# Second FFN of a macaron block: rows gathered per tile by GpSimd, against rows scattered to slots in DRAM and loaded by SyncE

## Chip, core and metric

One core of one Trainium2 chip. The metric is the device time of one execution in microseconds (us), the median of 3 runs. Five engines have programs of their own: TensorE (PE in the trace, its weight loads PEld), VectorE (DVE), ScalarE (ACT), GpSimd (POOL) and SyncE (SP, here only an issuer of DMAs).

## What is computed

The input x is 2 x 2048 tokens of 256 features in fp32, 4096 tokens in all. Three steps follow each other:

```python
x = x + 0.5 * ffn(layernorm(x))
x = x + attention(layernorm(x))
x = x + 0.5 * ffn(layernorm(x))

def ffn(xf):                      # xf: (4096, 256)
    scores = softmax(xf @ gate_w.T)            # 16 experts in 4 groups
    # two groups by the sum of their two best of (scores + gate_b), in them the two best experts
    weights, idx = the two chosen of scores
    h = silu(einsum('td,edi->tei', xf, We1) + be1) * (einsum('td,edi->tei', xf, We3) + be3)
    y = sum over the two experts of weight * (h @ We2 + be2)        # i = 128
    z = silu(xf @ ws1 + bs1) * (xf @ ws3 + bs3) @ ws2 + bs2          # shared, 256 wide
    return y + z
```

The attention is causal with 16 heads; a head's scores are products of six-element vectors (exterior products of two projections of four), and its values are 16 wide.

## The kernel before

Every token's residual row stays in SBUF (`x_res`, 32 tiles of 128 tokens; in blocks of `BT` = 4 tiles, so 8 blocks). The kernel is one program per engine, written out by hand; semaphores alone order the engines, and each engine and each DMA queue works its instructions in the order in which they stand.

**Attention** (`attend`) runs in 8 groups of 48 strips. For each strip TensorE makes scores (L1877), ScalarE their exponentials (L2017), GpSimd masks the strips on the diagonal (L2027), and TensorE multiplies with the values (L1903). Query chunks `qc` of 512 tokens end at fixed strips. Steps of other work are put between strips by tables of (group, strip) numbers: `turn_at`, `logits_at`, `count_at` (the second FFN's routing), `late_at` (turns of the last block of the lines, from the stage ahead of attention), `PROJECT_7` and `PROJECT_6_LATE` (the output projection L1917, whose product VectorE adds to `x_res` in L2097). `GATE` is 4, the first group in which the finished first half of the tokens may be normalized and routed. Normalized rows go to DRAM (`xn_rows`), a block of 4 tiles in a transfer (512 KB).

**The second FFN** (`ffn_by_halves`) works in two halves of 2048 tokens. Its slots: each (token, k) pair has a slot number, sorted by expert with every expert's share filled up to whole tiles of 128, which gives 47 tiles a half, 94 **turns**. `Routing.place` computes an offset per expert (`offset`) and the slot of each pair (`sum_slots`). A tile needs the tokens of its slots, so the map must be inverted: VectorE marks for each pair its row in the tile (`mark_rows`, L1152) and its tile (`mark_tiles`, L1158; `mark_of_pairs`, L1163; `scale_tiles`, L1167), TensorE multiplies the marks (`invert`, 32 small matmuls accumulated), and VectorE turns the product into token numbers (`name_tokens`). For half 0 the marks are made in the last attention group (`add_among_marks`), for half 1 inside turns 4 to 23, with the inversion at turn 26.

The loop over turns, as each engine sees it: GpSimd gathers the 128 rows of a turn from `xn_rows` with an indirect DMA (`bring`, L2499) into a ring of 16 tiles and, from turn 40, 8 more lent from `f_region`, the buffer of the marks. TensorE turns the rows (L2379), multiplies them with the expert's two up weights (L2391, 8 matmuls a turn) and the product down (L2403). ScalarE and VectorE copy, add biases and apply the gate between them; VectorE also copies each tile's expert weights by a register index (`take_weights`). SyncE stores each result tile to DRAM (`y_half`, L2292) from a ring of `ROUND` = 4. Once half 0 is stored, GpSimd gathers its results back for each token (`bring_back`, L2507), two gathers a tile of tokens, 32 for half 0 among the gathers of turns from turn 77 on (`BACK_TURN`), and VectorE adds them (`combine`, at the turns in `COMBINE_AT`). Half 1's results are gathered after the last turn, in the tail, together with the shared part (`shared_up`, L2560); `out` is stored by SyncE (L2296).

## Time and profile before

| what | value |
|---|---|
| median of 3 runs (lowest, highest) | 1233.25 us (1230.09, 1234.88) |
| the profiled execution's own time | 1235.22 us |
| its span in the trace | 1233.5 us |
| TensorE busy | 1046.1 us, 85% |
| VectorE busy | 772.3 us, 63% |
| ScalarE busy | 873.3 us, 71% |
| GpSimd busy | 457.8 us, 37% |

"Busy" counts the time of instructions that compute, for GpSimd also the time in which it writes the descriptors of an indirect DMA. It is an average over stages; which engine bounds a stage is read from that stage's window.

How the rows further down are read. A row of windows has, in this order: from and to (us from the start of the span), their length, then the busy us of PE, PEld, DVE, ACT and POOL with the number of records in brackets, the granted TensorE clock as a share of full speed, the mean busy share of the 16 DMA engines, and the GB/s that they moved. With a line chosen, only PE and PEld remain, which are the engines that run it. A row of the timeline has its start, its busy us, the engine, the line, output<-input with shapes, and in square brackets how long the engine was idle before it and what released it; "remote" is a release by something the trace doesn't name, "issue" is no wait that it shows. A row of groups has count, busy us, mean ns, and after the second bar the group's idle time with its releasers. A row of DMA queues has packets, MB and the share of 16 engines' span; a row of DMA issues ends with the size and the median us from issue to landing.

### The profile page before, as it was taken

The numbers are of one execution on the slowest core, as the hardware profiler recorded it, in microseconds if no ns is written. First come the engines' busy times: TensorE is split into PE (matmuls) and PEld (weight loads), VectorE is DVE, ScalarE is ACT, GpSimd is POOL, SyncE is SP. The second block draws the span as 40 slices with busy tenths as digits, with TensorE's granted clock in tenths as the row PEclk, the third lists the DMA queues.
The fourth block names the chain that finished last, engine by engine and source line by source line (L and its number), as shares of the span: only waits on it lengthen the run. The fifth ranks groups of instructions, "written<-read, shape, count | busy, mean of one in ns | idle before, by whom it ended". The sixth has DMA issues, their size and how long they took to land.

```text
span 1233.5 us, 23530 instructions
## 1 busy us (share of the span) xinstructions
PE 1046.1 (85%) x7487; PEld 570.4 (46%) x7487; DVE 772.3 (63%) x1565; ACT 873.3 (71%) x1250; POOL 457.8 (37%) x675
## 2 busy tenths in 40 slices
PE   3998999877887688988898989897999886967894
PEld 3457888744555212222222222221245685957752
DVE  6897777665997423444355565675786873645845
ACT  4246776624878999999999999999972463745610
POOL 1004555375630324331313234313133446564363
PEclk8999999998989799999999999999999997998997
DMA  8902544443756211010101130201009443443453
GB/s 294 279 4 78 161 152 156 130 127 108 219 176 213 88 31 52 18 52 18 52 18 53 35 104 19 74 15 52 2 31 318 127 137 124 155 137 114 131 167 120
DMA packets 125717, 133.79 MB, mean 108 GB/s; under 512 B 13224, under 2 KB 111888, under 8 KB 125616
## 3 DMA queue, kind: packets, MB, share of 16 engines
q1 hardware_dynamic: 109056, 90.95, 23.2%
q0 software_dynamic: 14448, 39.47, 11.1%
q10 hardware_dynamic: 2112, 2.10, 0.5%
q8 instruction: 55, 0.90, 0.3%
q14 instruction: 46, 0.38, 0.1%
HBM read 80.43 MB, written 52.04 MB: 107 GB/s over the span
## 4 chain that ended last, share of the span: by engine, by line
PE 30%; ACT 23%; issue 14%; DVE 7%; another core or an unknown queue 4%; DVEq 1%; ACTq 0%
ACT wide L2017 19%; PE banks L1903 6%; PE banks L2391 5%; PE banks L2316 3%; PE banks L2403 2%; PE banks L1877 2%; PE banks L2325 2%; PE banks L1433 2%; PE banks L1436 1%; PE banks L2379 1%; PE banks L1362 1%; DVEq L2599 1%; PE banks L1420 1%; PE banks L1917 1%
## 5 line engine op out<-in xcount | busy, mean ns | idle before, releaser
L2017 ACT ACTIVATE wide<-banks 128x1536 f32<-128x1536 f32 (+1 forms) x384 | 492.6, 1475 | 9.9 <-PE banks L1877 8.5
L1903 PE MATMUL banks<-wide,attn_attend_v_now 128*32 128x512 f32 (+3 forms) x2560 | 290.9, 546 | 1.9 <-ACT wide L2017 1.0
L2027 POOL TENSOR_SCALAR_AFFINE_SELECT wide<-wide 128x256 f32<-128x256 f32 (+1 forms) x320 | 115.3, 389 | 398.9 <-ACT wide L2017 396.4
L1877 PE MATMUL banks<-attn_attend_q_now,attn_attend_k_now 32*128 32x512 f16 (+3 forms) x1280 | 151.6, 357 | 55.6 <-ACT wide L2017 52.6
L1877 PEld LDWEIGHTS banks<-attn_attend_q_now,attn_attend_k_now 32*128 32x128 f16 x1280 | 38.8, 91 | 292.7 <-ACT wide L2017 243.2
L2391 PE MATMUL banks<-f_xnt 128*128 128x128 f32 x752 | 108.3, 290 | 39.0 <-ACT f_xnt L2476 19.2
L651 POOL DMA_INDIRECT f_region<-xn_rows,f_token_of x79 | 77.3, 978 | 137.1 <-DVE f_token_of L882 84.8
L2391 PEld LDWEIGHTS banks<-f_xnt 128*128 128x128 f32 x752 | 97.3, 202 | 46.5 <-ACT f_xnt L2469 25.3
L2072 DVE COPY sums<-banks 128x512 f32<-128x512 f32 x32 | 22.1, 692 | 141.9 <-PE banks L1903 141.6
L2077 DVE RECIPROCAL below<-below 128x512 f32<-128x512 f32 x32 | 107.3, 3353 | 1.1
L2499 POOL DMA_INDIRECT last_rows_in<-xn_rows,f_spare x72 | 69.6, 967 | 78.1 <-DVE f_stage L2560 24.5
L520 PE MATMUL banks<-f_region,wide 128*128 128x128 f32 x632 | 86.5, 280 | 6.4 <-issue 3.4
L1903 PEld LDWEIGHTS banks<-wide,attn_attend_v_now 128*32 128x32 f32 x2560 | 57.0, 109 | 75.1 <-issue 72.7
L520 PEld LDWEIGHTS banks<-f_region,wide 128*128 128x128 f32 x632 | 78.0, 194 | 10.1 <-issue 6.7
L2469 ACT ACTIVATE f_xnt<-last_w_all 128x514 f32 x94 | 59.4, 632 | 30.2 <-issue 23.7
L2483 ACT ACTIVATE f_xnt<-banks,f_xnt 128x128 f32<-128x128 f32 x94 | 34.3, 364 | 55.4 <-PE banks L2391 37.6
L1341 POOL DMA_INDIRECT f_region<-y_slots,attn_lines_rows_of x64 | 64.0, 1000 | 23.6 <-issue 17.1
L2610 DVE TENSOR_TENSOR f_xnt<-banks,last_w_down 128x256 f32<-128x256 f32 x94 | 39.4, 419 | 47.7 <-PE banks L2403 27.9
L619 ACT ACTIVATE wide<-f_w_all 128x514 f32 x79 | 49.9, 632 | 26.7 <-issue 23.6
L2403 PE MATMUL banks<-last_w_down,f_more 128*128 128x256 f32 x188 | 59.1, 397 | 1.0 <-DVE f_more L2617 1.0
L2097 DVE TENSOR_TENSOR x_res<-banks,x_res 128x512 f32<-128x512 f32 x30 | 20.7, 690 | 61.9 <-PE banks L1917 61.8
L2602 DVE COPY last_w_down<-last_w_all 128x512 f32 x94 | 41.5, 441 | 27.3 <-issue 23.8
(365 smaller groups left out, 1799.6 us busy)
## 6 DMA issues: line engine op xcount, KB each, us to landing
y_half<-f_xnt SPq DMA_DIRECT2D x94, 128.0 KB
y_slots<-wide SPq DMA_DIRECT2D x79, 128.0 KB
attn_v<-f_more SPq DMA_DIRECT2D x32, 256.0 KB
attn_attend_v_now<-attn_v SPq DMA_DIRECT2D x32, 256.0 KB, 3.3
x_res<-L_attn_x SPq DMA_DIRECT2D x8, 512.0 KB, 7.6
xn_rows<-f_w_all SPq DMA_DIRECT2D x8, 512.0 KB, 4.5
attn_q<-attn_lines_q_out SPq DMA_DIRECT2D x8, 512.0 KB
attn_k<-attn_lines_k_out SPq DMA_DIRECT2D x8, 512.0 KB
```

The source lines that it names most:

```text
L520: last = pe.matmul(bank[2 + m][:, f * P:(f + 1) * P], w_up[:, at, col_at:col_at + INTER], rows_t[:, m, c * P:(c + 1) * P], start=(c == 0), ...
L651: pool.indirect_dma_start(out=rows_in[:, n % ROUND, :], out_offset=None, in_=xn_rows, in_offset=bass.IndirectOffsetOnAxis(ap=token_of[:, n ...
L1341: pool.indirect_dma_start(out=back[:, q, j, k, :], out_offset=None, in_=y_slots, in_offset=bass.IndirectOffsetOnAxis(ap=rows_of[:, q, j, k ...
L1877: last = pe.matmul(score[i % SLOTS][:, j, column:column + columns(u)], k_now[rows, kt * P:(kt + 1) * P], q_now[rows, qc * QW + c0:(qc + 1) ...
L1903: last = pe.matmul(out_bank[qc][rows, c0:QW], v_now[:, kt, rows], probs[:, place, column:column + columns(u)], start=(kt == 0), stop=(u == ...
L2017: act.activation(probs_flat[:, at:at + width_of[i]], score_flat[i % SLOTS][:, 0:width_of[i]], ACT.Exp, scale=SCALE).then_inc(sem.exp_done, 1)
L2027: pool.affine_select(out=part, in_=part, compare_op=ALU.is_ge, fill=0.0, base=0, pattern=[[0, part.shape[1]], [1, P]], channel_multiplier= ...
L2077: dve.reciprocal(below[:], below[:]).then_inc(sem.chain_step, 1)
L2391: last = pe.matmul(bank[2 + m][:, f * P:(f + 1) * P], w_up[:, at, col_at:col_at + INTER], rows_t[:, m, c * P:(c + 1) * P], start=(c == 0), ...
L2403: pe.matmul(bank[4 + m][:, 0:D], prod_t[:, at, :], w_down[:, at, 0:D], start=True, stop=True).then_inc(sem.y_done, 1)
L2469: act.activation(w_up[:, n % ROUND, :], w_all[:, bass.ds(expert, 1), 0:UP].rearrange("p o f -> p (o f)"), ACT.Copy).then_inc(sem.up_kept, 1)
L2499: pool.indirect_dma_start(out=rows_in(n), out_offset=None, in_=xn_rows, in_offset=bass.IndirectOffsetOnAxis(ap=s.token_of[:, place_of_turn ...
```

## The change

The inversion goes. In its place the rows themselves are scattered: GpSimd writes the 128 rows of a tile of tokens to their slots in DRAM (`x_slots0`, `x_slots1`, 47 x 128 rows of 1 KB each), one indirect DMA for each of the 32 (tile, k) pairs of a half (`send`), and SyncE loads each turn's 128 rows from there with one plain transfer (`load_rows`), into a ring of 8 tiles, the next one behind each store of a result. The slots that no pair fills must hold something finite: SyncE clears both tensors with two transfers of zeros ahead of the loads of attention group 2 (`clear`). The normalized rows are loaded back from `xn_rows` into `f_region` ahead of the scatters (`fetch_rows`: four transfers of 512 KB a half, for half 1 at turn 4). Half 0 is sent in bursts of 7, 14, 4, 4 and 3 (`SENT`), the first two in the last attention group, the others ahead of the loop; half 1 follows at once in one burst of 32. The gathers of half 0's results then stand alone in the loop (turn 57 on for `combine`, one every other turn). The addition of the shared bias to half 1 moves from behind the loop, as 4 instructions, into turns 7 to 21, as 8. In attention, slots of half 0 are computed a group earlier, and turns, projections and copies move to other strips.

```diff
-    def place_pairs(self, dve, half):
-        for k in range(TOPK):
-            self.sum_slots(dve, k)
-        self.split_slots(dve)
...
-    def mark_rows(self, dve, first, pairs):
-        s = self.s
-        some = slice(first, first + pairs)
-        row_id = self.core.row_id[:].rearrange("p (o m) -> p o m", o=1).to_broadcast([P, pairs, P])
-        row_of = s.row_of[:, some].rearrange("p (q o) -> p q o", o=1).to_broadcast([P, pairs, P])
-        dve.tensor_tensor(s.row_hot[:, some, :], row_id, row_of, ALU.is_equal)
...
-    def name_tokens(self, dve, half, bank):
...
+    def clear(self, sp, x_slots):
+        sp.wait_ge(self.s.sem.zeros_made, 1)
+        for slots in x_slots:
+            sp.dma_start(dma_rows(slots), self.s.zeros.rearrange("p (o d) -> p o d", o=1).to_broadcast([P, HALF_TURNS, D])
+                         ).then_inc(self.s.sem.cleared, 16)
+
+    def fetch_rows(self, sp, half, xn_rows):
+
         s = self.s
-        dve.wait_ge(s.sem.inverted, half + 1)
-        dve.tensor_scalar(s.token_f, bank[:, HS:2 * HS], float(P), float(half * HT * P - 1), ALU.mult, ALU.add)
-        self.step(dve, dve.scalar_tensor_tensor(s.empty_f, bank[:, 0:HS], 0.0, self.core.part_one[:].to_broadcast([P, HS]), ALU.is_equal, ALU.mult))
-        self.step(dve, dve.tensor_tensor(s.token_f, s.token_f, bank[:, 0:HS], ALU.add))
-        dve.tensor_tensor(s.token_of[:, half * HS:(half + 1) * HS], s.token_f, s.empty_f, ALU.add).then_inc(s.sem.tokens_ready, 1)
+        sp.wait_ge(s.sem.slots_ready, half + 1)
+        if half == 0:
+            for q in range(2):
+                sp.wait_ge(s.stored[q], 16 * HB // 2)
+        else:
+            for q in range(2):
+                sp.wait_ge(s.stored[q], 16 * (BLOCKS - 2) // 2)
+            sp.wait_ge(s.stored[2], 16 * 2)
+            sp.wait_ge(s.sem.sent, 16 * HP)
+        for b in range(HB):
+            first = half * HT + b * BT
+            sp.dma_start(s.rows_out[:, b * BT:(b + 1) * BT, :], dma_rows(xn_rows)[:, first:first + BT, :]).then_inc(s.fetched[b], 16)
+
+    def send(self, pool, half, first, end, x_slots):
+
+        s = self.s
+        if half == 0 and first == 0:
+            pool.wait_ge(s.sem.cleared, 16 * 2)
+        for pair in range(first, end):
+            t, k = pair // TOPK, pair % TOPK
+            if pair == first or pair % (BT * TOPK) == 0:
+                pool.wait_ge(s.fetched[t // BT], 16 * (half + 1))
+            at = half * HT + t
+            pool.indirect_dma_start(out=x_slots[half], out_offset=bass.IndirectOffsetOnAxis(ap=self.core.slots[:, at, k:k + 1], axis=0),
+                                    in_=s.rows_out[:, t, :], in_offset=None).then_inc(s.sem.sent, 16)
...
-    def invert(self, pe, half, bank):
-        s = self.s
-        pe.wait_ge(s.sem.hot_ready, half + 1)
-        for q in range(HP):
-            last = pe.matmul(bank[:, 0:2 * HS], s.row_hot[:, q, :], s.tile_hot[:, q, :, :].rearrange("p a s -> p (a s)"),
-                             start=(q == 0), stop=(q == HP - 1))
-        last.then_inc(s.sem.inverted, 1)
...
-PROJECT_7, PROJECT_6, PROJECT_6_LATE = (22, 25), (34, 38, 42, 45), (39, 41, 43, 45)
+PROJECT_7, PROJECT_6, PROJECT_LATE = (22, 25), (34, 38, 42, 45), (25, 28, 38, 41, 43, 45)
...
-               (GATE + 1, 10): (2, 0), (GATE + 1, 13): (2, 1), (GATE + 1, 18): (3, 0), (GATE + 1, 20): (3, 1)}
-    weights_at, logits_at, logits_turn_at, count_at, exp_at = (GATE, 34), (GATE + 1, 34), (GATE + 1, 38), (GATE + 2, 45), (GATE + 2, 4)
...
+               (GATE + 1, 10): (2, 0), (GATE + 1, 13): (2, 1), (GATE + 1, 21): (3, 0), (GATE + 1, 23): (3, 1)}
+    weights_at, logits_at, logits_turn_at, count_at, exp_at = (GATE, 34), (GATE + 1, 34), (GATE + 1, 36), (GATE + 2, 42), (GATE + 2, 4)
...
-    late_at = {(0, 3): 0, (0, 5): 1, (0, 9): 2, (0, 11): 3}
...
+    late_at = {(0, 18): 0, (0, 20): 1, (0, 22): 2, (0, 25): 3}
+    late_bank = banks[:, 7, :]
+    copied_at = (0, 4)
...
+            if g == 2:
+                routing.clear(sp, x_slots)
...
+        routing.fetch_rows(sp, 0, xn_rows)
...
+                if u == last_of[0] and g == 1:
+                    pool.memset(second.zeros, 0.0).then_inc(second.sem.zeros_made, 1)
+                if u == last_of[1] and g == GATE + 3:
+                    routing.send(pool, 0, 0, SENT[0], x_slots)
...
                 if u == last_of[2] and g == GATE + 3:
                     routing.take_root(pool, HB, BT)
+                    routing.send(pool, 0, SENT[0], SENT[1], x_slots)
...
                 routing.weigh(dve, 0)
                 routing.keep_counts(dve, 0, rest_bank(count_at[1]))
                 dve.sem_inc(sem.rest_kept, 1)
-            elif g == GATE + 3 and qc == 0:
                 routing.place(dve, 0)
-            elif g == GATE + 3 and qc == 1:
                 routing.name_experts(dve, 0)
...
-        def add_among_marks(two):
+        def add_last_chunks(two):
 
             routing.normalize(dve, HB)
             add_half(two, 1, 0)
-            routing.mark_rows(dve, 0, HP)
-            routing.mark_tiles(dve)
             add_half(two, 1, 1)
             sum_block(two, 1)
-            routing.mark_tokens(dve)
             add_half(two, 2, 0)
...
-ROWS, LENT, LENT_FROM = 16, 8, 40
+SENT = (7, 21, 25, 29)
+ROWS = 8
...
+        def load_rows(n):
+            if n >= ROWS:
+                sp.wait_ge(sem.rows_turned, n - ROWS + 1)
+            half, at = n // HALF_TURNS, n % HALF_TURNS * P
+            sp.dma_start(rows_in[:, n % ROWS, :], x_slots[half][at:at + P, :]).then_inc(row_loaded[n % ROWS], 16)
+
+        sp.wait_ge(before.proj_added, ends.adds)
+        sp.wait_ge(first.sent, 16 * HP)
+        for n in range(ROWS):
+            load_rows(n)
         for n in range(TURNS):
+            if n == 4:
+                routing.fetch_rows(sp, 1, xn_rows)
+            if n + ROWS == HALF_TURNS:
+                sp.wait_ge(first.sent, 16 * 2 * HP)
             sp.wait_ge(sem.y_ready, n + 1)
             sp.dma_start(y_halves[n // HALF_TURNS][n % HALF_TURNS * P:(n % HALF_TURNS + 1) * P, :], y_rows[:, n % ROUND, :]).then_inc(row_stored[n % ROUND], 16)
+            if n + ROWS < TURNS:
+                load_rows(n + ROWS)
...
-            if n == INVERT_AT:
-                routing.invert(pe, 1, bank[6])
...
         routing.take_root(pool, HB + 1, BT)
+        routing.send(pool, 0, SENT[1], SENT[2], x_slots)
         routing.take_root(pool, HB + 2, BT)
-        pool.wait_ge(first.tokens_ready, 1)
-        pool.wait_ge(before.pv_done, ends.values)
-        for n in range(4):
...
-        for n in range(ROWS, TURNS):
-            if n == LENT_FROM:
-                pool.wait_ge(first.inverted, 2)
-            if n == HALF_TURNS:
-                pool.wait_ge(first.tokens_ready, 2)
-            bring(n)
...
-            pair = n - BACK_TURN
-            if pair == 0:
-                for q in range(ROUND):
-                    pool.wait_ge(row_stored[q], stored_by(q, HALF_TURNS))
-            if pair >= 0:
-                bring_back(pair // TOPK, pair % TOPK)
-        for pair in range(TURNS - BACK_TURN, HP):
-            bring_back(pair // TOPK, pair % TOPK)
+        pool.wait_ge(s.stored[0], 16 * (BLOCKS - 2) // 2)
+        pool.wait_ge(s.stored[1], 16 * (BLOCKS - 2) // 2)
+        for t in range(HT):
+            for k in range(TOPK):
+                bring_back(t, k)
...
+        dve.wait_ge(first.sent, 16 * HP)
...
+        def add_shared_bias(i):
+            pair = x[:, HT + 2 * i:HT + 2 * i + 2, :]
+            dve.tensor_tensor(pair, pair, s.bs2.rearrange("p (o d) -> p o d", o=1).to_broadcast([P, 2, D]), ALU.add).then_inc(first.bs2_added, 1)
...
-        SOME = HP // 8
-        rows_at = {n: SOME * i for i, n in enumerate((6, 7, 9, 10, 12, 13, 15, 16))}
+        bs2_at = {7 + 2 * i: i for i in range(HT // 2)}
         for n in range(TURNS + 3):
             if n in (2, 3):
                 routing.sum_slots(dve, n - 2)
             if n == 4:
-                routing.split_slots(dve)
-            if n == 5:
                 routing.name_experts(dve, 1)
-            if n in rows_at:
-                routing.mark_rows(dve, rows_at[n], SOME)
-            if n in (18, 19):
-                routing.mark_tiles(dve, (n - 18) * HP // 2, HP // 2)
-            if n in (20, 21):
-                routing.mark_of_pairs(dve, (n - 20) * HP // 2, HP // 2)
-            if n == 22:
-                routing.scale_tiles(dve, 0, HP // 2)
-            if n == 23:
-                routing.scale_tiles(dve, HP // 2, HP // 2).then_inc(first.hot_ready, 1)
-            if n == INVERT_AT + 3:
-                routing.name_tokens(dve, 1, bank[6])
+            if n in bs2_at:
+                add_shared_bias(bs2_at[n])
...
-        for b in range(HB, BLOCKS):
-            part = x[:, b * BT:(b + 1) * BT, :]
-            dve.tensor_tensor(part, part, s.bs2.rearrange("p (o d) -> p o d", o=1).to_broadcast([P, BT, D]), ALU.add).then_inc(first.bs2_added, 1)
-        dve.wait_ge(first.bs2_added, BLOCKS)
+        dve.wait_ge(first.bs2_added, HB + HT // 2)
...
-INVERT_AT, BACK_FIRST, BACK_RING = 26, 4, 2 * BT
+BACK_FIRST, BACK_RING = 4, 2 * BT
...
-BACK_TURN = HALF_TURNS + ROWS + LENT + 6
-COMBINE_AT = (61, 64, 67, 70, 73, 76, 79, 82, 84, 85, 87, 88, 90, 92, 93, 95)
+COMBINE_AT = range(HALF_TURNS + 10, HALF_TURNS + 10 + 2 * HT, 2)
```

Three places show how instructions move. GpSimd from the last masks of attention to the first results gathered back (`f_spare` is the root of the variance, `f_region` and `last_rows_in` the two parts of the ring), before:

```order
L2027 AFFINE_SELECT wide<-wide 128x128
L1021 TENSOR_TENSOR f_spare<-f_spare 128x4 x2
L2499 DMA last_rows_in<-xn_rows,f_spare 128x256 x4
L1021 TENSOR_TENSOR f_spare<-f_spare 128x4
L2499 DMA last_rows_in<-xn_rows,f_spare 128x256 x36
L2499 DMA f_region<-xn_rows,f_spare 128x256 x8
L2499 DMA last_rows_in<-xn_rows,f_spare 128x256 x16
L2499 DMA f_region<-xn_rows,f_spare 128x256 x8
L2499 DMA last_rows_in<-xn_rows,f_spare 128x256 x6
L2507 DMA f_stage<-y_half,slots 128x256
```

and after:

```order
L2011 AFFINE_SELECT wide<-wide 128x128
L1018 TENSOR_TENSOR f_spare<-f_spare 128x4
L1172 DMA x_slots<-f_region,slots 6016x256 x4
L1018 TENSOR_TENSOR f_spare<-f_spare 128x4
L1172 DMA x_slots<-f_region,slots 6016x256 x4
L1018 TENSOR_TENSOR f_spare<-f_spare 128x4
L1172 DMA x_slots<-f_region,slots 6016x256 x35
L2479 DMA f_stage<-y_half,slots 128x256 x32
L2479 DMA last_w_all<-y_half,slots 128x256 x32
```

The 94 gathers of rows are gone; the last 3 scatters of half 0 and the 32 of half 1 stand in one run, and the 64 result gathers follow with nothing between them.

VectorE in the last attention group, between the last chunk's normalization and the statistics of the added block, before:

```order
L1036 TENSOR_SCALAR f_stage<-x_res,f_spare 128x256 x4
L2097 TENSOR_TENSOR x_res<-banks,x_res 128x512
L1152 TENSOR_TENSOR f_region<-row_id,f_spare 128x4096
L1158 TENSOR_TENSOR f_region<-tile_id,f_spare 128x32x48
L2097 TENSOR_TENSOR x_res<-banks,x_res 128x512
L152 BN_STATS parts<-x_res 128x6 x4
```

and after:

```order
L1033 TENSOR_SCALAR f_stage<-x_res,f_spare 128x256 x4
L2086 TENSOR_TENSOR x_res<-banks,x_res 128x512 x2
L152 BN_STATS parts<-x_res 128x6 x4
L1002 TENSOR_TENSOR f_spare<-parts 128x4
L1003 TENSOR_TENSOR f_spare<-parts 128x4
```

The two marks between the two additions are gone, so the additions follow each other.

SyncE from the last expert weights (`last_w_all`) to the output, before:

```order
L2288 DMA last_w_all<-L_ffn_We 128x16x256
L2289 DMA last_w_all<-L_ffn_be 128x16x256
L2292 DMA y_half<-f_xnt 128x256 x94
L2296 DMA out<-x_res 128x4x256 x7
L2296 DMA out<-x_res 128x2x256
```

and after, up to the store of turn 4:

```order
L2253 DMA last_w_all<-L_ffn_We 128x16x256
L2254 DMA last_w_all<-L_ffn_be 128x16x256
L2260 DMA last_rows_in<-x_slots 128x256 x8
L2272 DMA y_half<-f_xnt 128x256
L2260 DMA last_rows_in<-x_slots 128x256
L2272 DMA y_half<-f_xnt 128x256
L2260 DMA last_rows_in<-x_slots 128x256
L2272 DMA y_half<-f_xnt 128x256
L2260 DMA last_rows_in<-x_slots 128x256
L2272 DMA y_half<-f_xnt 128x256
L2260 DMA last_rows_in<-x_slots 128x256
L1160 DMA f_region<-xn_rows 128x4x256 x4
```

Loads of rows now alternate with the stores of results in one queue, and the four reloads of half 1 stand ahead of the store of turn 4 and all behind it.

## Rows read from the trace of the kernel before

**Rows 1.** Windows by stage, columns as told in the section on the profile.
```profile
403.00:915.00 512.00, 450.70 (x4075) 124.40 (x4075) 271.33 (x381) 498.19 (x392) 149.69 (x337) 0.98 0.13 40
915.00:966.80 51.80, 50.43 (x194) 29.85 (x193) 39.56 (x91) 15.47 (x25) 16.67 (x17) 1.00 0.75 241
966.80:1015.00 48.20, 40.48 (x299) 35.88 (x297) 38.90 (x106) 31.02 (x76) 23.52 (x24) 1.00 0.41 127
1015.00:1050.00 35.00, 23.68 (x162) 20.99 (x161) 12.86 (x38) 14.08 (x34) 19.44 (x21) 0.80 0.37 117
1050.00:1080.00 30.00, 29.44 (x225) 27.03 (x225) 20.46 (x55) 21.24 (x54) 18.39 (x20) 1.00 0.52 164
1080.00:1140.00 60.00, 43.20 (x283) 38.44 (x282) 30.68 (x83) 29.52 (x71) 32.25 (x34) 0.91 0.42 126
1140.00:1172.40 32.40, 28.78 (x201) 24.65 (x200) 26.30 (x73) 19.63 (x49) 12.65 (x13) 1.00 0.43 129
1172.40:1233.50 61.10, 44.09 (x128) 24.78 (x126) 30.62 (x54) 5.39 (x8) 31.14 (x32) 0.86 0.46 143
```

**Rows 2.** The same windows of the loop for line 2391 alone (8 records a turn).
```profile
966.80:1015.00 48.20, 27.27 (x200) 24.25 (x200) 1.00 0.41 127
1015.00:1050.00 35.00, 14.51 (x86) 13.36 (x87) 0.80 0.37 117
1050.00:1080.00 30.00, 19.79 (x149) 17.95 (x149) 1.00 0.52 164
1080.00:1140.00 60.00, 28.73 (x190) 25.98 (x190) 0.91 0.42 126
1140.00:1172.40 32.40, 18.01 (x132) 15.79 (x130) 1.00 0.43 129
```

**Rows 3.** The chain that ended last, two turns: start, us, what.
```profile
1057.28 0.89 PE banks L2391 x8
...
1058.82 0.89 PE banks L2391 x8
```

**Rows 4.** GpSimd's groups in the loop: busy us, mean ns, idle before and its releasers.
```profile
L2499 POOL DMA_INDIRECT last_rows_in<-xn_rows,f_spare x56 | 54.2, 968 | 41.5 <-PE banks L2379 24.2 <-issue 10.8 <-DVE x_res L2552 3.4
```

**Rows 5.** Timeline of one stall: start, us, engine, line, [idle before <-releaser].
```profile
1036.48 0.95 POOL L2499 DMA_INDIRECT last_rows_in<-xn_rows,f_spare  x1 [0.30 <-issue]
...
1038.75 0.37 ACT L2483 ACTIVATE f_xnt<-banks,f_xnt 128x128 f32<-128x128 f32 x1 [4.20 <-remote]
1038.79 0.42 DVE L2610 TENSOR_TENSOR f_xnt<-banks,last_w_down 128x256 f32<-128x256 f32 x1 [3.62 <-remote]
```

**Rows 6.** Timeline of VectorE, a mark inside a turn.
```profile
999.80 0.95 DVE L1158 TENSOR_TENSOR f_region<-tile_id,f_spare 128x768 bf16<-128x768 bf16 x1
```

**Rows 7.** Timeline of the last attention group.
```profile
884.23 1.02 POOL L1021 TENSOR_TENSOR f_spare<-f_spare 128x4 f32<-128x4 f32 x1 [3.87 <-DVE f_spare L1011]
...
895.00 4.41 DVE L1152 TENSOR_TENSOR f_region<-row_id,f_spare 128x4096 bf16<-128x4096 bf16 x1
...
901.98 0.65 POOL L2027 TENSOR_SCALAR_AFFINE_SELECT wide<-wide 128x256 f32<-128x256 f32 x2 [16.73 <-ACT wide L2017]
...
907.69 1.10 PE L1917 MATMUL banks<-attend_w_o,heads 128*128 128x256 f32 x4 [1.86 <-DVE x_res L2097]
...
909.16 2.99 ACT L2017 ACTIVATE wide<-banks 128x1536 f32<-128x1536 f32 x2 [1.28 <-PE banks L1877]
```

**Rows 8.** DMA: the hardware queue, and a wide window under full load.
```profile
q1 hardware_dynamic: 109056, 90.95, 23.2%
...
925.00:962.00 37.00, 36.35 (x133) 19.94 (x132) 26.30 (x67) 8.57 (x14) 9.98 (x11) 1.00 0.94 303
...
xn_rows<-f_w_all SPq DMA_DIRECT2D x8, 512.0 KB, 4.5
```

**Rows 9.** SyncE's queue between attention groups 2 and 3.
```profile
539.73 29.92 SPq L1786 DMA_DIRECT2D attn_attend_q_now<-attn_q  x4
```

**Rows 10.** Timeline of VectorE's longest wait in the tail.
```profile
1205.87 0.75 DVE L2560 SCALAR_TENSOR_TENSOR f_stage<-banks,last_bs,f_more 128x512 f32<-128x512 f32 x1 [12.82 <-remote]
```

118 lines of the change are left out of this document (35 added, 83 removed).

## Prediction, written before the changed kernel was run

> **What bounds the kernel now.** I read the windows by stage first [rows 1]; one row is one stretch, and its first columns are the busy time of TensorE, its weight loads, VectorE, ScalarE and GpSimd. Attention (403 to 915) is ScalarE's: 498.19 busy of 512.00 us. From 915 to the start of the loop over turns TensorE is busy 50.43 of 51.80 us. The loop itself (five windows, 205.6 us) belongs to nobody: at best TensorE fills 29.44 of 30.00 us, at worst 23.68 of 35.00. The reader is to see that the loop has one good window and four bad ones with the same work per turn.
>
> How much is lost there comes from line 2391 alone, 8 records a turn [rows 2]: 200, 86, 149, 190 and 132 records are 25, 10.75, 18.6, 23.75 and 16.5 turns. Undisturbed, two turns stand 1058.82 - 1057.28 = 1.54 us apart in the chain of waits [rows 3]. At 1.545 us a turn the windows would take 38.6, 16.6, 28.8, 36.7 and 25.5 us; they take 9.6, 18.4, 1.2, 23.3 and 6.9 us more, **59.4 us lost in all**. (94 turns at 1.545 us are 145.2 us.)
>
> What goes with the losses is GpSimd. A gather occupies it 0.95 us and 0.30 us pass to the next [rows 5], so at most one goes out per 1.25 us. In the good window it issues 20 [rows 1] in 30 us, one a turn, each held back by the ring. In the window 1015 to 1050 it issues 21, all but a few of them back to back, and from 1080 to 1140 34, because gathers for the turns and gathers of finished results share it: 2 x 1.25 = 2.5 us a turn against 1.545. In such a burst ScalarE and VectorE then stand still together for 4.20 and 3.62 us on something the trace calls remote, although TensorE has nothing long to do [rows 5]; the granted clock of the stretch falls to 0.80 between the two levels of 1.2 and 2.4 GHz [rows 1], after TensorE had stood idle. That is a correlation and not yet a cause: bursts lose 18.4/21 = 0.88 us per indirect transfer in one window and 23.3/34 = 0.69 in the other, paced ones 1.2/20 = 0.06.
>
> The tail (61.1 us) has the same picture: a burst of gathers, and VectorE waits 12.82 us on remote [rows 10]. The change leaves that burst in place.
>
> **The change part by part.** *GpSimd in the loop.* Before, 78 of the 94 row gathers (56 of them into the own ring [rows 4], 22 into the lent one) and 32 result gathers fall into the loop, 110 x 1.25 = 138 us of issue. After, 32 scatters and 32 gathers, 64 x 1.25 = 80 us. No scatter is in the trace; the nearest row is the gather of the same 128 rows of 1 KB, 0.95 us [rows 5], and I take that for it (both ends: a descriptor list of 128 rows is built either way, and a scatter at twice the price, 64 + 80 = 144 us in all, would only restore the old load). Result gathers no longer alternate with row gathers: their pairs take 2.5 us per two turns (3.1 us). So the 23.3 and 6.9 us of the last two windows shrink. I leave 8 us for them: the first eight go as one burst (8 x 0.69 = 5.5), the 24 paced ones cost 24 x 0.06 = 1.4, and 1 for the two additions, about 1 us per two turns, that VectorE must place in slack.
>
> *The burst of 32 scatters* for the second half replaces the one at 1015 to 1050. Priced like a paced transfer it loses 32 x 0.06 = 2 us, like the gather burst 32 x 0.88 = 28 us. The 18.4 us it replaces include the inversion on TensorE, whose 32 small matmuls go. I take 16 us, 0.5 a scatter, in between: it is a burst like those, but no turn waits for a row that GpSimd has yet to fetch. SyncE also puts 2.1 MB of row reloads (4 x 512 KB) ahead of the stores of turn 4 and later. The queue moved 90.95 MB in 23.2% of 1233.5 us, 318 GB/s while busy [rows 8], so that is 6.6 us; the ring of four result rows covers 6.2 us less the landing, so 3 us.
>
> *VectorE in the loop* loses its marks: a mark of tiles takes 0.95 us in a turn [rows 6] and four such turns overrun; of the 9.6 us in the first window I leave 5 for the offset steps, which stay. Eight additions of the shared bias come in at turns 7 to 21, of 128x512 each, one per two turns; the nearest row is the mark's 0.95 us. The cover is what VectorE has free, 9.5 us in 18.6 turns of the good window [rows 1, 2], about 1 us in two turns; without it they cost 8 x 0.95 = 7.6 us. The third window keeps its 1.2, and 4 us stay for what I cannot name. Loop after: 5 + 16 + 3 + 1 + 8 + 4 = 37 us lost instead of 59, **-22 us**.
>
> *Last attention group.* The marks of half 0 stand on VectorE between additions: 4.41 us for the first alone; TensorE's projection then waits 1.86 us for an addition and ScalarE idles 1.28 us [rows 7]. Gone: **-1.3 us**. GpSimd gets 7 and 14 scatters here. The 14 follow the root that ends at 885.25 and take 17.5 us, to 902.75; the masks start at 901.98 after 16.73 us of idleness [rows 7]. They come 0.8 us late and are needed some strips later, so 0. The moved steps in attention (turns of the last line block, projections, logits, counts) keep their number: they take from the 512.00 - 498.19 = 13.8 us that ScalarE is not busy, **-1 us** (0 to -3).
>
> *Clearing.* SyncE writes 2 x 47 x 128 rows of 1 KB, 12.3 MB, after the last load for group 2, whose issue begins at 539.73 [rows 9]. At 318 GB/s this is 39 us; the window 925 to 962 shows 303 GB/s with TensorE busy 36.35 of 37.00 us under it [rows 8]. A group lasts 512/8 = 64 us, and group 2 has just begun, so group 3 starts at about 602 and the clear is hidden with some 20 us to spare: 0.
>
> *Before the loop and in the tail.* TensorE's matmuls between 915 and 967 stay; the inversion of half 0 goes, but beside it VectorE's last chunk runs anyway: 0. The loads of the first eight tiles queue behind the expert weights and wait for all 32 scatters of half 0: 0, at worst 3. In the tail four bias additions of 128x1024 leave VectorE while TensorE has the matmuls of two blocks ahead: 0. If that cover were gone they would give up to 4 x 2 x 0.95 = 7.6.
>
> Sum: 22 + 1.3 + 1 = 24 us off the span of 1233.5, so 1209.2; the profiled run took 1235.2, 2.0 above the median of 1233.25, so the same 24 us off the median give **1209 us**.
>
> **Two rules against the rows.** The good window has a DMA share of 0.52 and the burst window 0.37 [rows 1]: the engines are not full where the loop stands still. The Trainium skill, DMA: Bandwidth & Descriptors, section on queues, rings and completion order, says that each DMA engine takes turns between the queues that have work, packet by packet. By that rule a burst of GpSimd's would hardly hold up SyncE's stores, and the rows do not agree, unless the wait is for something else. The same page, section on issuing engines that are not separate DMA queues, says that starting transfers from another engine saves only the time to start them. The trace agrees that this time is what GpSimd spends; for the bytes it speaks against the change.
>
> **The rivals.** *A, bursts like the paced transfers.* The low DMA share in the burst window speaks for it, the 4.20 us waits against. The 16 and 3 us shrink to 2: 1192 us. (The page's taking of turns would have this outcome.)
>
> *B, the DMA engines become the bound of the loop.* Loop transfers of 128 KB: before 94 stores + 78 + 32 gathers = 204, after 94 stores + 94 loads + 32 scatters + 32 gathers + 16 of reload = 268, 35 MB, 110 us at 318 GB/s in a loop of 182. For: loads and stores share one queue and the rings hold eight rows instead of 16 to 24. Against: 110 is below 145. If each fetched row and store comes late for a third of the turns by half a microsecond, 15 us return: 1224 us. (The second rule of the page points here.)
>
> *C, scatters of half 0 hurt attention or the start.* 21 transfers at 0.5 us stalls of ScalarE's stream, partly hidden: +6, 1215 us. Against: ScalarE and TensorE wait for no DMA in the last group.
>
> *D, the clear is too slow, the other side.* Writes of 512 KB to DRAM land 4.5 us after issue [rows 8], 117 GB/s with the latency in it. At that rate the clear lasts 105 us and the loads of group 3 stand behind it: 105 + 540 = 645 against 602, 43 us of stall, 1252 us. It stalls from 12.3 MB / 62 us = 199 GB/s down; it turns the sign from 12.3 / (62 + 24) = 143 GB/s.
>
> **How the numbers follow.** Main case 0.48 (1199 to 1222), A 0.20, B 0.14, C 0.10, D 0.08. The range from 1186 to 1230 takes in the main case, A, B and C, whose bounds reach 2 and 28 us for the burst; D lies outside. Half a per cent (6 us, about what can be told from no change) ends at 1227: faster 0.48 + 0.20 + 0.10 and half of B, 0.85; within 0.5% the rest of B, 0.07; slower D, 0.08.
>
> **What would show it.** The loop from its first row transpose to its last product takes about 182 us instead of 205.6; GpSimd shows 32 transfers of 0.95 us in a row early in it, and stalls on remote lie inside that burst and not between turns 47 and 94. The third attention group keeps its length, DMA share near 1 for 39 us at 540. VectorE's first additions in group 7 have no gap over 2 us. The prediction is wrong if a scatter occupies GpSimd much longer than 0.95 us, if TensorE waits for a row that SyncE loaded, or if group 3 starts late.

## The result: 1246.3 us against 1232.2, slower by 1.0%

Four runs of the changed kernel take 1244.04 to 1248.74 us, median 1246.33; the kernel before, four runs now, has 1232.2. The ratio is 1.0099, 95% interval 1.0073 to 1.0125. The forecast was 1209. On other chips the sign is the other one (0.990, below); this section is about the first kind of chip, on whose trace the prediction was made.

The profiled execution took 1247.99 us, span 1246.3, 12.8 more than before. Four landmarks split these 12.8. Attention, from its first to its last exponential, took 506.9 us (403.8 to 910.7) and takes 516.6 (405.3 to 921.9): **+9.7**. From there to the first row transpose of the loop it was 56.2 and is 58.6: **+2.4**. The loop took 205.1 (966.9 to the last product at 1172.0) and takes 204.1 (980.5 to 1184.6): **-1.0**. The tail was 61.5 and is 61.7, and attention starts 1.5 later. The forecast was 37 us below this span: 12 of them are attention (-2.3 us was forecast), 21 the loop (-22).

Windows of the changed kernel, with the columns of [rows 1]: the last attention group, the stretch before the loop, six parts of the loop, the tail.

```profile
861.00:922.00 61.00, 48.49 (x374) 13.05 (x374) 23.83 (x50) 45.43 (x35) 31.54 (x47) 0.86 0.13 46
922.00:980.00 58.00, 54.48 (x214) 32.51 (x207) 40.46 (x95) 16.93 (x27) 11.76 (x12) 0.94 0.70 224
980.40:998.00 17.60, 14.64 (x109) 12.81 (x107) 14.10 (x41) 11.55 (x28) 0.00 (x0) 1.00 0.28 90
998.00:1045.00 47.00, 15.62 (x75) 13.22 (x73) 8.35 (x21) 7.03 (x17) 30.64 (x32) 0.66 0.47 163
1045.00:1104.00 59.00, 58.26 (x430) 54.21 (x431) 41.90 (x113) 43.20 (x111) 0.00 (x0) 0.95 0.54 162
1104.00:1120.00 16.00, 10.72 (x64) 9.61 (x63) 5.65 (x16) 6.66 (x17) 7.73 (x8) 0.79 0.55 163
1120.00:1163.00 43.00, 40.88 (x305) 36.60 (x305) 36.97 (x101) 30.40 (x76) 23.52 (x24) 1.00 0.76 216
1163.00:1185.00 22.00, 21.33 (x156) 18.90 (x155) 17.24 (x48) 14.67 (x37) 0.32 (x1) 1.00 0.50 151
1185.00:1246.30 61.30, 44.48 (x129) 24.80 (x127) 25.71 (x49) 5.39 (x8) 30.49 (x32) 0.88 0.46 143
```

The same six parts of the loop for the up product alone (L2371, 8 records a turn), as in [rows 2]:

```profile
980.40:998.00 17.60, 9.93 (x72) 8.72 (x72) 1.00 0.28 90
998.00:1045.00 47.00, 9.84 (x48) 9.08 (x48) 0.66 0.47 163
1045.00:1104.00 59.00, 39.96 (x288) 36.66 (x288) 0.95 0.54 162
1104.00:1120.00 16.00, 7.14 (x41) 6.67 (x42) 0.79 0.55 163
1120.00:1163.00 43.00, 27.32 (x204) 24.59 (x205) 1.00 0.76 216
1163.00:1185.00 22.00, 13.65 (x103) 12.13 (x101) 1.00 0.50 151
```

At 1.545 us a turn they lose 3.7, **37.7**, 3.4, 8.1, 3.6 and 2.1 us. The 47 us in which GpSimd issues the 32 scatters of half 1 hold 6 turns. GpSimd is at 30.64 us there, TensorE at 15.62 and VectorE and ScalarE under 9, the DMA engines at 0.47. In the 59 us behind it, with nothing on GpSimd, TensorE is busy 58.26.

What the engines wait for inside that run is in its timeline (start, us, engine, line, what, [idle before it and releaser]):

```profile
1008.59 1.72 PE L2371 MATMUL banks<-f_xnt 128*128 128x128 f32 x8
...
1010.14 0.60 PE L2383 MATMUL banks<-last_w_down,f_more 128*128 128x256 f32 x2
...
1010.58 0.38 PE L2359 MATMUL banks<-ident,last_rows_in 128*128 128x128 f32 x2
...
1013.17 0.38 ACT L2454 ACTIVATE f_xnt<-banks 128x256 f32<-128x256 f32 x1 [4.34 <-issue]
...
1015.50 1.06 PE L2383 MATMUL banks<-last_w_down,f_more 128*128 128x256 f32 x2
...
1016.35 0.61 PE L2359 MATMUL banks<-ident,last_rows_in 128*128 128x128 f32 x2
...
1025.84 0.37 ACT L2461 ACTIVATE f_xnt<-banks,f_xnt 128x128 f32<-128x128 f32 x1 [12.28 <-remote]
...
1031.43 0.42 DVE L2568 TENSOR_TENSOR f_xnt<-banks,last_w_down 128x256 f32<-128x256 f32 x1 [18.64 <-remote]
...
1031.88 0.32 SPq L2272 DMA_DIRECT2D y_half<-f_xnt  x1
...
1037.04 0.38 ACT L2454 ACTIVATE f_xnt<-banks 128x256 f32<-128x256 f32 x1 [9.60 <-remote]
1037.53 2.05 PE L2371 MATMUL banks<-f_xnt 128*128 128x128 f32 x8 [20.57 <-issue]
1038.08 0.96 POOL L1172 DMA_INDIRECT x_slots<-f_region,slots  x1 [0.30 <-issue]
```

Each of these lines has its 94 turns in the trace, so a product and its reader can be matched by counting. The up product of turn 12 was done at 1010.3, and ScalarE, which reads it, starts at 1025.84, 15.5 us later. The down product of turn 10 was done at 1010.7, and VectorE starts on it at 1031.43, 20.7 us later. The transpose of turn 14 was done at 1011.0, and ScalarE starts on it at 1037.04, 26.1 us later. (What TensorE did at 1015.50 and 1016.35 belongs to turns 11 and 15 and was read later still.) The releases come 5.6 us apart (1025.84, 1031.43, 1037.04). The trace also records when a semaphore is raised. Those of these three products are raised at 1025.81, 1031.41 and 1037.02, just ahead of the starts; in the turns before the run they are raised 0.014 us behind the end of the product. So the readers were ready, and the notice came late.

The other way there is no delay: VectorE's result of 1031.4 is stored by SyncE at 1031.88, and 0.1 us behind ScalarE's copy of 1037.04 TensorE starts. ScalarE's two instructions wait for no DMA; VectorE's addition also waits for an older store, but it starts when TensorE's semaphore is raised. It is TensorE's own signals that arrive late. One reservation: the trace models the end of a matmul, so it can't tell a late signal from a product that was itself finished late. That TensorE went on to the products of turns 13, 11 and 15 in the meantime speaks for the signal.

The first late ones are the down product of turn 9, done at 1008.4 and read 2.7 us later, and the transpose of turn 13, done at 1008.8 and copied at 1013.17, 4.4 us later. Eight scatters of the run that starts at 998.97 had been issued by then.

In attention, where nothing needs a scatter, the run of 14 does the same:

```profile
902.79 1.13 PE L1899 MATMUL banks<-attend_w_o,heads 128*128 128x256 f32 x4
903.73 0.96 POOL L1172 DMA_INDIRECT x_slots<-f_region,slots  x1 [0.31 <-issue]
906.63 4.13 ACT L2001 ACTIVATE wide<-banks 128x1536 f32<-128x1536 f32 x3 [4.22 <-remote]
906.90 0.69 DVE L2086 TENSOR_TENSOR x_res<-banks,x_res 128x512 f32<-128x512 f32 x1 [9.51 <-remote]
```

The projection of 902.79 was done at 903.9 and is added at 906.90, 3.0 us late; in [rows 7] ScalarE's longest idleness in the same group was 1.28 us. The clearing is as forecast. The rows are the page's for the two transfers, their landing times, and the window of that group:

```profile
x_slots<-f_spare SPq DMA_DIRECT2D x2, 6016.0 KB, 30.1
...
DMA to landing us min/median/max: 21.7/30.1/38.5
...
531.00:595.00 64.00, 55.35 (x528) 13.98 (x521) 24.79 (x24) 63.91 (x51) 13.69 (x40) 1.00 0.68 227
```

The first of the two lands 21.7 us after its issue at 538.8 and the second 38.5 us after its issue at 539.3, so the clear lasts 39 us; the 30.1 is only the mean of the two. ScalarE is busy 63.91 of 64.00 us meanwhile.

The reloads of half 1 cost what was forecast for them. The view of `x_slots` gives the row loads and, under who waited for them:

```profile
L2260 SPq DMA_DIRECT2D last_rows_in<-x_slots x94: 424/432/5802, 962.8 to 1175.9; - x94
...
  PE banks L2359: 3.9, 1
```

That is TensorE's transpose of turn 12, which waits until 1005.12 for a row whose load stands behind the reloads. In the same stretch VectorE waits 3.5 us for the store of turn 4, until 1004.93. These two are DMA waits and not late signals.

### The profile page after: what moved, and what is told of

It is laid out like the page before. It is cut to its first block, busy times and chain, and to the rows that moved or that the text cites. A ratio compares the mean times of both kernels' runs of the same rounds, so it can differ in the third digit from the quotient of the medians.

```text
span 1246.3 us, 23449 instructions
## 1 busy us (share of the span) xinstructions
PE 1047.1 (84%) x7423; PEld 569.4 (46%) x7423; DVE 753.3 (60%) x1533; ACT 871.0 (70%) x1250; POOL 426.7 (34%) x646
## 4 chain that ended last, share of the span: by engine, by line
PE 30%; ACT 24%; issue 13%; another core or an unknown queue 7%; DVE 4%; POOL 1%; DMA 1%; DVEq 0%; ACTq 0%; POOLq 0%
ACT wide L2001 20%; PE banks L1885 6%; PE banks L2371 6%; PE banks L2298 4%; PE banks L1859 3%; PE banks L2383 3%; PE banks L2307 1%; PE banks L2359 1%; PE banks L1899 1%; PE banks L1400 1%; PE banks L1413 1%; PE banks L1416 1%; DVE x_res L1575 1%; POOL f_region L1321 1%
## 5 line engine op out<-in xcount | busy, mean ns | idle before, releaser
L2371 PE MATMUL banks<-f_xnt 128*128 128x128 f32 x752 | 107.8, 290 | 38.8 <-issue 30.6
L2371 PEld LDWEIGHTS banks<-f_xnt 128*128 128x128 f32 x752 | 97.9, 203 | 43.9 <-issue 36.7
L1172 POOL DMA_INDIRECT x_slots<-f_region,slots x64 | 62.4, 975 | 72.8 <-DMA f_region<-xn_rows 54.3
L2086 DVE TENSOR_TENSOR x_res<-banks,x_res 128x512 f32<-128x512 f32 x30 | 20.7, 691 | 89.4 <-PE banks L1899 78.8
L2479 POOL DMA_INDIRECT f_stage<-y_half,slots x32 | 31.6, 986 | 92.7 <-DMA y_half<-f_xnt 65.1
L2383 PE MATMUL banks<-last_w_down,f_more 128*128 128x256 f32 x188 | 58.6, 395 | 0.4 <-DVE f_more L2575 0.4
## 6 DMA issues: line engine op xcount, KB each, us to landing
x_slots<-f_spare SPq DMA_DIRECT2D x2, 6016.0 KB, 30.1
```

The costliest lines, as they stand in the source:

```text
L1172: pool.indirect_dma_start(out=x_slots[half], out_offset=bass.IndirectOffsetOnAxis(ap=self.core.slots[:, at, k:k + 1], axis=0), in_=s.rows_ ...
L2371: last = pe.matmul(bank[2 + m][:, f * P:(f + 1) * P], w_up[:, at, col_at:col_at + INTER], rows_t[:, m, c * P:(c + 1) * P], start=(c == 0), ...
L2383: pe.matmul(bank[4 + m][:, 0:D], prod_t[:, at, :], w_down[:, at, 0:D], start=True, stop=True).then_inc(sem.y_done, 1)
```

## The experiments

Theory S is what the timeline suggests: an unbroken run of indirect DMAs on GpSimd delays TensorE's signals, and the same transfers apart from each other do not.

**e1, scatters of the loop one per turn.**

```diff
-        routing.send(pool, 1, 0, HP, x_slots)
+        for pair in range(HP):
+            pool.wait_ge(sem.rows_turned, 7 + 1 * pair)
+            routing.send(pool, 1, pair, pair + 1, x_slots)
```

> The changed kernel, but GpSimd issues the 32 scatters of half 1 one per turn (pair p after turn 7 + p has been transposed) and not in one run. Theory S (signals): an unbroken run of indirect DMAs on GpSimd makes TensorE's completion signals reach ScalarE and VectorE late, from about the seventh transfer on, some 5.6 us apart; apart from each other they cost next to nothing. It expects the stretch that now takes 50 us for 7 turns to lose under 5 us, and 1205 to 1217 us in all against 1246. Rival W (work of the transfers: each scatter takes its toll whenever it is issued): the same 32 scatters cost about the same spread out, 1236 to 1248. Rival R (reloads and stores: the stall is that of the SyncE queue behind the four reloads of 512 KB at turn 4): the stall stays where it is, 1240 to 1248.

1213.92 us, ratio to before 0.985 (0.979 to 0.991; the kernel before 1234.66 in these runs). The loop takes 174.4 us against 204.1. The window that holds the same 32 scatters, all engines and then L2371:

```profile
993.00:1050.00 57.00, 48.95 (x368) 44.22 (x367) 37.49 (x100) 36.45 (x91) 31.21 (x32) 1.00 0.78 250
...
993.00:1050.00 57.00, 32.63 (x244) 29.61 (x245) 1.00 0.78 250
```

It holds 30.5 turns in 57 us where the run left 6 in 47, with GpSimd as busy and twice the DMA share. W and R fall: neither the scatters' own work nor the queue behind the reloads, which stand where they stood, made the stall. The 57 us still lose 9.9 us (57 - 30.5 x 1.545), more than the 5 that S allowed. The first seven scatters still go out nearly as a run (998.03 to 1005.85), because the turns that they wait for had already been transposed, and beside them a transpose is copied 3.1 us after its end; 3 us more are the reloads'.

**e2, scatters in attention apart.** The first 21 of half 0 go one at a time after strips 5, 7, 9, ..., 45.

```diff
-                    routing.send(pool, 0, 0, SENT[0], x_slots)
...
-                    routing.send(pool, 0, SENT[0], SENT[1], x_slots)
...
+            while g == GATE + 3 and sent[0] < SENT[1] and SEND_AT[sent[0]] < strip:
+                pool.wait_ge(sem.exp_done, N * g + SEND_AT[sent[0]] + 1)
+                routing.send(pool, 0, sent[0], sent[0] + 1, x_slots)
+                sent[0] += 1
```

> The changed kernel, but its first 21 scatters of half 0 are spread over the last attention group, one after every second strip from strip 5 on, where they were issued as runs of 7 and 14. Attention there ended 9.7 us later than in the kernel before (by its own start). Theory S: the runs are the cause, spread out 8 to 10 us return, 1236 to 1239. Rival W: nothing returns, 1244 to 1248. Rival M (the moved steps made the groups longer, not the scatters): nothing returns either, 1244 to 1248, and the last group stays 10 us too long with no signal that is late.

1224.85 us, ratio 0.990 (0.983 to 0.997). Attention takes 503.5 us instead of 516.6, 13.1 less and 3.4 less than before the change. Five of the 21 still go in a run (883.12 to 888.25, GpSimd had stood at a root before), and ScalarE's waits in the group are 3.5 us in all, against 15.3 in the changed kernel and 3.4 before: this run of five did no harm. W and M fall; S had 8 to 10 us and 1236 to 1239, which is too little. By the medians 21 us return, in the traces 15.5 (1246.3 to 1230.8): the four executions spread from 1215.2 to 1232.59, and the profiled one is the slowest. The 13.1 us of attention are the firmer number.

**e3, narrow rows.**

```diff
-            pool.indirect_dma_start(out=x_slots[half], ..., in_=s.rows_out[:, t, :], in_offset=None)
+            pool.indirect_dma_start(out=self.narrow[half], ..., in_=s.rows_out[:, t, 0:64], in_offset=None)
```

> The changed kernel, but every scatter writes only the first 64 of a row's 256 numbers, into tensors that nobody reads (the turns load the cleared slots, so the routed part of the second FFN is computed from zeros). As many scatters of as many rows, a quarter of the bytes. Theory S: what counts is the number of transfers issued in a row, so the time stays, 1240 to 1250. Rival B (bytes: the scattered data hold up SBUF or the DMA engines): most of the 39 us lost in the run of 32 and of the 10 us in attention return, 1200 to 1220.

1243.80 us, ratio 1.008 (1.005 to 1.010): with a quarter of the bytes nothing returns (attention 518.1 us, loop 209.7). B falls.

**e4, the moved steps alone.** Before, with the tables of the change (`PROJECT_LATE`, `turn_at`, `late_at` and what hangs on them).

> The kernel before with only the moved steps of attention (turns and copies of the last line block at strips 18 to 25, projections, turns, logits, counts of group 5 and 6); gathers, marks and inversion as before. Theory S: the moves cost or bring nothing, 1230 to 1235. Rival M: the moves cost up to 10 us in attention, 1238 to 1243.

1233.05 us, ratio 0.9985 (0.995 to 1.002). In the trace attention takes 503.9 against 506.9. M falls.

**e5 to e7, both spread, and two variants.** e5 joins e1 and e2. e6 adds `pool.wait_ge(sem.rows_turned, 52 + TOPK * t + k)` ahead of each result gather. e7 sends half 1 by `range(0, HP, 8)` in runs of 8. **e8** is a kernel of signals alone; its core, where `made` is one of the kinds of transfer:

```python
for r in range(ROUNDS):                                   # TensorE
    if p or r:
        pe.wait_ge(sem["act_done"], ROUNDS * p + r)
    pe.matmul(bank[:, 0:P], left[:], kept[:], start=True, stop=True).then_inc(sem["pe_done"], 1)
...
act.wait_ge(sem["pe_done"], rounds_before(p, False) + r + 1)    # ScalarE
act.copy(sink[:], bank[:, 0:P]).then_inc(sem["act_done"], 1)
...
for n in range(RUN):                                      # GpSimd, in a run
    ...
    made.then_inc(sem[which(p)], 16)
```

> The changed kernel with the scatters of both experiments apart from each other: the 21 of half 0 one after every second strip of the last attention group, the 32 of half 1 one per turn. Theory S: the two returns lie in different stages and add up, 13 us in attention (503.5 against 516.6 us from first to last exponential) and 30 us in the loop (170.3 against 200.0), so 1246 - 43 = 1203, 1198 to 1208. Rival H (the start or the tail takes back what attention gives, since row loads wait for something else): 1210 to 1216, no better than the loop alone.

> As the kernel with both paced, and the gathers of half 0's results also at most one per turn from turn 52 on, where the first eight were issued in one run, beside which the changed kernel's turns took 7 us too long. Theory S: gathers in a run are no better than scatters, 4 to 7 us return against the kernel with both paced. Rival G (only scatters delay signals, gathers do not): within 1 us of it.

> As the kernel with both paced, but the 32 scatters of half 1 go in four runs of 8, one run every 8 turns: the same mean rate as one per turn. Theory S with a threshold: the first six or so of a run are free and only the seventh and eighth come late, so at most two late signals a run, 4 x 2 us or less, 1203 to 1212. Rival A (the mean rate counts, not the run): equal to both paced. Rival F (every transfer of a run costs, no threshold): 32 x 0.9 = 29 us of the 30 are lost again, 1225 to 1235.

> A kernel of its own that computes nothing of the reference and stores the input as output. TensorE (a 128x128 matmul) and ScalarE (a copy of its product) signal each other 40 times in each of nine phases: with nothing beside it; with 20 gathers of 128 rows of 1 KB issued in a run; the same with rows of 256 bytes; one gather per round; 20 plain transfers of 128 KB started by GpSimd; the same started by SyncE; gathers of 1 KB while VectorE and ScalarE signal each other; 20 scatters of 1 KB rows; 20 gathers of 32 rows. Theory S: rounds of TensorE and ScalarE stretch from about 1 us to several us from about the seventh gather or scatter of a run on, at either row size, and not in the phases with nothing, with paced gathers and with plain transfers; signals of VectorE stay prompt. Rival B (bytes): plain transfers stretch the rounds as well, narrow rows do not. Rival V (all engines' signals): the phase of VectorE stretches too.

These, and e9 to e12, ran on another chip than e1 to e4: there the kernel **before** takes 1161.69 us. e5 1149.87, ratio 0.990 (0.987 to 0.992); e6 1153.14, 0.992 (0.989 to 0.994); e7 1151.80, 0.992 (0.990 to 0.994). No row of the three traces waits on remote, and in e8 (407.71 us, one execution) each round of TensorE and ScalarE keeps its 1.15 us beside every kind of transfer. So e6 and e7 told nothing of signals here, and the question became whether the chip decides.

**e9 to e12, the changed kernel on the second chip.**

> The changed kernel once more, unchanged. The last four runs were on another chip, on which the kernel before took 1161.7 us and not 1233, and on which no engine waited over a microsecond for a signal beside a run of transfers. If late signals are a property of a chip, the ratio to the kernel before depends on it: on a chip with the kernel before at about 1233 us it is 1.010, on one at 1162 us it is 0.985 to 0.995 (the changed kernel near the one with both sets paced, 1150). Rival K (the cause is in the kernels and not in the chip): 1.010 on any chip.

> The kernel with both sets of scatters paced, beside the changed kernel on one chip. On a chip with late signals 1198 to 1208 us against 1246 for the changed kernel; on one without them within 4 us of the changed kernel.

> Half 1's scatters in four runs of 8, for a chip with late signals: with a threshold at six transfers 0 to 8 us above both paced; if each transfer of a run costs 0.9 us, 25 to 30 us above. On a chip without late signals equal to both paced.

> The kernel of signals alone (it computes nothing of the reference) with runs of 32 transfers and 60 rounds a phase. On the chip of the last four runs every round of TensorE and ScalarE took 1.15 us, with 20 gathers in a run beside it too. On a chip with late signals theory S expects the rounds to stretch from the seventh transfer on, in the phases with runs of gathers or scatters and in no other; if the rounds stay at 1.15 us although the changed kernel is slow, it takes more than a run of transfers beside a light engine.

The kernel before took 1162.28 us. Changed 1149.52, **0.990 (0.987 to 0.993)**; both paced 1149.48, 0.991 (0.988 to 0.994); runs of 8 1150.91, 0.991 (0.989 to 0.993). K falls: the same program is 1.0% slower on one chip and 1.0% faster on the other. Of the 32 scatters in one run there, in the trace of e9, the window and its L2371:

```profile
951.00:992.00 41.00, 37.51 (x277) 34.51 (x276) 28.50 (x75) 27.57 (x70) 31.43 (x32) 0.96 0.87 286
...
951.00:992.00 41.00, 25.29 (x184) 23.21 (x184) 0.96 0.87 286
```

GpSimd is as busy as in the 47 us above and issues just as fast; 23 turns go by and not 6. In e12 (one execution), with runs of 32, each of the 480 products of TensorE is read within 0.3 us of its end.

**e13 to e15, signals alone on the first kind of chip.**

> The kernel of signals alone, runs of 32, once more in the hope of a chip of the first kind (kernel before at about 1233 us). There theory S expects rounds of 1.15 us to stretch to several us in the phases with runs of gathers or scatters; if they stay at 1.15 us it takes more than a run of transfers beside a light TensorE. On a chip of the second kind (1162 us) all rounds stay at 1.15 us.

> Both sets of scatters paced. On a chip of the first kind 1198 to 1208 us, 0.97 to 0.98 of the kernel before; on one of the second kind 0.990 again.

> The kernel before, profiled once more. On a chip of the second kind its loop over turns should show no wait on remote and take some 205.6 - 59 + 10 = 155 to 170 us, since the 59 us lost in it on the first chip lay beside runs of gathers; its tail should lose the 12.8 us wait of VectorE. On a chip of the first kind it repeats the trace at hand.

This is a third chip. The kernel before took 1244.85 us on it, so it is of the first kind. Signals alone, again one execution: 691.01 us against 612.88 for the same program in e12. ScalarE beside the run of 32 gathers that starts at 75.83 (timeline of e13):

```profile
94.16 0.27 ACT L119 COPY sink<-bank 128x128 f32<-128x128 f32 x1 [0.88 <-issue]
...
99.25 0.27 ACT L119 COPY sink<-bank 128x128 f32<-128x128 f32 x1 [2.52 <-remote]
...
102.75 0.27 ACT L119 COPY sink<-bank 128x128 f32<-128x128 f32 x1 [3.24 <-remote]
...
107.65 0.27 ACT L119 COPY sink<-bank 128x128 f32<-128x128 f32 x1 [4.63 <-remote]
...
118.15 0.27 ACT L119 COPY sink<-bank 128x128 f32<-128x128 f32 x1 [5.33 <-remote]
```

Rounds go from 1.15 us to 3.5, to 4.9 and at the end to 5.6 us, the spacing seen in the kernel. The first late signal is that of a product done at 97.6, when (97.6 - 75.8)/1.25, some 17 transfers, had gone out. Counted over the whole trace, 29 of the 480 products are read more than 0.3 us after their end: six in each of the phases with 1 KB gathers, 256-byte gathers, gathers one per round and scatters, five in that with gathers of 32 rows, and none in the others. From ScalarE to TensorE nothing is late: within a phase TensorE starts at most 0.49 us behind ScalarE's copy, in e13 as in e12. The waits of ScalarE in phases of e13, one window each (what it waited for: us in total, times, longest): the run of 1 KB gathers, of 256-byte gathers, one gather per round, and 32 plain transfers from GpSimd.

```profile
ACT sink L119 <- remote: 20.4, 5, 5.3
...
ACT sink L119 <- remote: 17.8, 4, 5.3
...
ACT sink L119 <- remote: 8.3, 3, 3.2
...
ACT sink L119 <- PE bank L98: 54.0, 61, 0.9
```

The width of a row does not count; plain transfers of the same bytes do nothing; scatters and gathers of 32 rows behave as gathers do (longest 4.6 and 5.3 us). One gather per round of 1.15 us is hardly slower than a run and is hit less, not spared: it takes more room than that. The phase of VectorE is touched lightly: at its end ScalarE idles 1.1 us a round instead of 0.3, 0.8 us in all for two signals, of which one or both are late. So V is right in part: something of VectorE's exchange is delayed too, but by far less.

Both paced has 1205.57 us, **0.966 (0.960 to 0.972)**, attention 503.6, loop 174.7: the parts add up, as S had it. e15 repeats before at 1244.43 (0.998, 0.995 to 1.002; loop 207.7).

**e16 to e18.**

> Half 1's scatters in four runs of 8, one run every 8 turns, for a chip of the first kind, where both paced gives 0.966 of the kernel before and a loop of 170 us. If the run decides and is harmful from about the fifth transfer (the changed kernel's run of 32 showed its first gap there), each run of 8 costs 2 to 6 us: 0.97 to 0.985. If the mean rate decides: 0.966. On a chip of the second kind 0.990.

> Both sets of scatters paced and the result gathers of half 0 at most one per turn. On a chip of the first kind 0.960 to 0.964 of the kernel before, 3 to 7 us below both paced, if runs of gathers are as bad as runs of scatters. On one of the second kind 0.990.

> The kernel before. On a chip of the second kind its loop over turns takes 155 to 170 us against 205.6 and shows no wait on remote over a microsecond; on a chip of the first kind it repeats the trace at hand.

A fourth chip, of the second kind (before 1161.41): 1150.48 and 0.991 (0.989 to 0.993); 1152.99 and 0.992 (0.990 to 0.995); before 1160.94 and 0.999 (0.998 to 1.001). Paced results were 2.5 to 3.3 us slower than the kernels beside them both times (e6 and e17; loop 162.3 and 161.9 us against 156.5 in e5 and 160.1 in e16), with intervals that overlap. Runs of 8 scatters and paced results were thus never tried where signals are late. e18 gave the missing trace. Its loop takes 164.2 us (942.5 to 1106.7) where the first chip needs 205.1, and no wait of the whole trace is on remote; gathers and marks are the same:

```profile
990.00:1025.00 35.00, 34.93 (x290) 32.30 (x289) 24.39 (x68) 25.62 (x65) 25.32 (x27) 1.00 0.61 175
```

27 indirect transfers in 35 us, TensorE busy throughout, beside [rows 1]'s 23.68 us with 21.

The two traces of the kernel before, on a chip of each kind, also say where the chips differ. The first 100 us of the span, in which GpSimd issues no indirect transfer yet (its first starts at 102.65), are the same, first kind and second kind:

```profile
0.00:100.00 100.00, 77.96 (x335) 48.21 (x335) 82.53 (x169) 43.11 (x115) 4.52 (x28) 0.97 0.56 178
...
0.00:100.00 100.00, 78.22 (x335) 48.42 (x335) 82.55 (x169) 43.12 (x115) 4.53 (x28) 0.97 0.56 178
```

Of the 74.0 us between the spans (1233.5 and 1159.5), 22.7 lie ahead of attention, 40.9 in the loop and 8.7 in the tail, the three stages with many indirect transfers. Attention, which has none, has 1.3, and the stretch before the loop, with its runs of four and eight gathers, 0.4. And the first FFN has such waits on the first kind of chip, while GpSimd gathers in a run:

```profile
267.37 1.06 PE L1397 MATMUL banks<-ident,f_stage 128*128 128x128 f32 x8 [1.88 <-ACT f_stage L225]
...
278.99 0.30 ACT L1483 ACTIVATE attn_lines_xt<-attn_lines_xt,attn_lines_goes_on 128x2 f32<-128x2 f32 x1 [11.77 <-remote]
```

ScalarE waits there for TensorE's transposes alone, done at 268.4, and starts 10.6 us later.

## Why the prediction was wrong

**What bounds the kernel: right in place, the cause left open.** The losses coincide with bursts, and so do the waits on remote. The prediction called this "a correlation and not yet a cause". e1, e2, e3 and e13 make it one for the first kind of chip: late signals beside runs of indirect transfers. If the chips differ in nothing else here, about 41 of the loop's 59 us lost are theirs: 205.1 less e18's 164.2. What on the chip delays them stays open.

**The burst of 32 scatters: the step that failed, a mis-sized term.** The prediction had its price from the trace, 0.88 us per transfer of a burst and 28 us in all as upper bound, and took 0.5 and 16 us, because "no turn waits for a row that GpSimd has yet to fetch". That reason names the data of the transfer, and the data are not what waits: TensorE's signals are, and every engine that reads a product stands still with them. Burst and reloads were put at 19 us; the window lost 37.7; against e1 the run costs 29.7, or 0.93 a scatter. So 0.88 was the measured row and held; the 3 us for the reloads lie in the remaining 8, and were right: the waits for the store of turn 4 (3.5 us) and for the row of turn 12 (3.9 us) run side by side, and on the second kind of chip e9 has the same wait for the store of turn 4, 3.1 us, there named as a wait for the DMA.

**Scatters in attention: the other step that failed, 0 forecast, 13 us measured** (516.6 against e2's 503.5). The sum asked only whether the masks come late. Rival C had the right mechanism, stalls of ScalarE's stream, half its size and 0.10; its "Against", that ScalarE and TensorE wait for no DMA in that group, was true and beside the point. At the same 0.88, 21 scatters would have been 18 us. The masks themselves were not late: after its run GpSimd stood idle for 7.92 us until ScalarE reached the next one, at 912.61. Sum with 0.88 throughout: 1209 + 12 + 18 = 1239, near what came.

**The rest of the loop: right.** 18 us were left besides burst and reloads, 20.9 are lost (3.7, 3.4, 8.1, 3.6, 2.1). The first eight result gathers cost 8.1 where 5.5 stood, the 24 paced ones and the additions little.

**Last attention group, moved steps: right.** 2.3 us forecast; 3.0 in e4's trace, 3.4 in e2's. **Clearing: right**, 39 us of transfer as forecast, 0 us of time; D, at 199 GB/s or less, did not happen. **Before the loop and tail:** 2.4 and 0.2 us against 0 (at worst 3).

**The signs.** Of what was to show the forecast, the 32 transfers in a row came (0.96 us each), and group 3 kept its length (61.4 us from its first exponential to the next group's). The loop took 204.1 us and not 182. Stalls on remote lay inside the burst, but also in the run of eight result gathers between turns 47 and 94 (ScalarE 3.21 us at 1111.19, VectorE 4.44 us at 1111.87), and VectorE's addition at 906.90 in the last group came after 9.51 us of idleness and not under 2, the last 3.0 of them behind the end of its product. Of the three signs of being wrong, only one came, TensorE's single wait of 3.9 us for a row, and it was priced. None of the three named what went wrong.

**Rivals A and B.** Of the rule that queues take turns (the Trainium skill, DMA: Bandwidth & Descriptors, queues, rings and completion order) the prediction said that the rows do not agree "unless the wait is for something else". It is: for TensorE's signals, so the rule is neither borne out nor contradicted. A would be near the second kind of chip, where a run costs about 7 us of loop (loop 164.0 in e9, 157.2 in e10). B did not happen: the 36 turns from 1045 to 1104 run at 0.54 DMA share with TensorE at 58.26 of 59.00.

**Sign on the second kind of chip.** The change is faster there by 12.8 us in the medians of e9 to e12. The traces at hand are of two chips of that kind, e18's of the kernel before and e9's of the changed one; they differ by 12.1 us, and not in the loop: 164.2 before, 164.0 after (931.9 to 1095.9). Most of the loss that the 22 us were to come from does not exist there. The gain lies in attention (505.6 before, 497.9 in e9, 499.8 to 504.5 in the seven traces with spread scatters there), 2.1 us ahead of it, 1.3 in the tail and 0.8 before the loop. How much of the 7.7 us in attention is the moved steps and how much is spread between executions is open.

## What to carry to other kernels

Price a run of indirect transfers by what every engine loses beside it, also one that needs none of its data, and take that price from the nearest run in the trace. Spread such transfers, one per turn or per second strip: with scatters it gave 3.4% against the kernel before on one kind of chip and cost nothing on the other. Match a late reader to its product by counting turns; the product that ended last before it is the wrong one here and would hide 6 us of the delay. Before explaining a stall, measure the kernel before on the chip in hand: a stall on one may not exist on the next.

## What the hardware showed unexpectedly

Four chips carried e1 to e18, and they are of two kinds: on two of them the kernel before takes 1235 and 1245 us, on the other two 1161 to 1162 (the result itself, with 1232, is of the first kind). The mean granted clocks of the two traces of the kernel before, 0.960 and 0.972 over the span, are too near for 6%. On the first kind, 32 indirect transfers 1.25 us apart delay TensorE's signals until they come 5.6 us apart. The delay set in after some 14 to 19 transfers of a run in the kernel of signals alone, and after eight in the loop. Shorter runs are not all harmless: beside the first seven scatters of e1 a transpose is copied 3.1 us after its end, and beside the run of eight result gathers of the changed kernel a down product is read 4.6 us after its end, with VectorE idle for 4.44 of them. The run of five in e2 and the runs of four and eight gathers ahead of the loop, in the kernel before, show no such loss. Signals of ScalarE to TensorE and of VectorE to SyncE were not late in the rows above. Whether a rate or a backlog sets in there, and what differs between the chips, are open: runs of 8 scatters met no chip of the first kind.
